# Block counts of the last layer: five cells per step beside each attention loop, in place of four and six

## What is computed

```python
x = _layernorm(x + L0(x, edge_index, edge_weight))       # weighted sum of neighbours
x = _layernorm(x + L1(x, edge_attr_32, edge_index, ...)) # attention, 4 heads, softmax over edges
x = _layernorm(x + L2(x, edge_index, ...))               # attention, 1 head, leaky relu
x = _layernorm(x + L3(x, edge_index, W1, b1, W2, b2))    # two graph convolutions:
# agg = segment_sum(x[col], row); agg/deg ; relu((agg/deg + x) @ W1 + b1), then again with W2
```

## Time and profile before

| what | us |
|---|---|
| median of 3 runs | 4830.54 (4828.19 to 4831.01) |
| the profiled execution | 4824.61, its span 4822.8 |
| first attention loop, from 1885 to 2980 | 1095 |
| second attention loop, from 3107 to 4440 | 1333 |
| everything else | 2394.8 |

### The profile page before, as it was taken

How to read it: one execution, slowest core, us unless ns; L and a number is a source line. 1 busy time by engine, 2 the same in 40 slices (tenths; PEclk the granted TensorE clock), 3 DMA queues, 4 the chain that set the end, 5 groups by cost and what they waited for, 6 DMA issues and landing times. The chain is left out here.

```text
span 4822.8 us, 75928 instructions
## 1 busy us (share of the span) xinstructions
PE 2356.4 (49%) x18851; PEld 1736.9 (36%) x18904; DVE 2781.6 (58%) x5419; ACT 647.4 (13%) x1473; POOL 2686.7 (56%) x2730
## 2 busy tenths in 40 slices
PE   0133333333306624666666665355555555555798
PEld 0023333333305513454544454233333333333232
DVE  8641111111118865777777777577877887877201
ACT  0001111111105410111111111011111111111000
POOL 0037777777745522777777774176666666663000
PEclk9955555555555555566666656555555555555899
DMA  0133334343315523555555552143333333332744
GB/s 21 38 123 124 125 122 130 126 129 123 114 36 109 107 47 85 140 144 148 143 147 147 143 146 78 42 102 94 94 95 91 91 97 92 94 95 60 275 170 168
DMA packets 533005, 537.07 MB, mean 111 GB/s; under 512 B 213790, under 2 KB 370324, under 8 KB 532618
## 3 DMA queue, kind: packets, MB, share of 16 engines
q1 hardware_dynamic: 243738, 289.79, 20.1%
q0 software_dynamic: 81072, 115.39, 10.7%
q10 hardware_dynamic: 208000, 130.01, 8.8%
HBM read 376.99 MB, written 159.58 MB: 111 GB/s over the span
## 5 line engine op out<-in xcount | busy, mean ns | idle before, releaser
L1381 POOL DMA_INDIRECT rows<-nodes_xl,id_slot x832 | 868.3, 1044 | 577.8 <-issue 240.9
L638 POOL DMA_INDIRECT msg_by_src<-message,place_slot x832 | 832.6, 1001 | 343.5 <-issue 252.8
L1381 POOL DMA_INDIRECT rows<-nodes_kv,id_slot x832 | 822.6, 989 | 339.8 <-issue 242.0
L1697 PE MATMUL counts_p<-hot_blocks 128*128 128x128 bf16 x2080 | 541.1, 413 | 362.3 <-DVE running_counts L1569 319.8
L599 PE MATMUL picked<-X,hotT 128*128 x1664 | 374.5, 423 | 674.2 <-issue 390.3
L599 PEld LDWEIGHTS picked<-X,hotT 128*128 128x128 f32 x1664 | 360.6, 331 | 688.0 <-issue 688.0
L560 DVE TENSOR_TENSOR message<-picked,w_dst 128x512 f32<-128x512 f32 x104 | 71.9, 691 | 845.7 <-ACT message L612 838.0
L1738 PE MATMUL sums<-parts,hot 128*128 128x68 bf16 (+1 forms) x4992 | 325.2, 251 | 374.9 <-DVE parts L1558 374.9
L1697 PEld LDWEIGHTS counts_p<-hot_blocks 128*128 128x128 bf16 x2080 | 277.5, 148 | 545.0 <-DVE running_counts L1569 339.1
L1738 PEld LDWEIGHTS sums<-parts,hot 128*128 128x128 bf16 x4992 | 311.8, 168 | 424.1 <-issue 424.1
L1569 DVE SCALAR_TENSOR_TENSOR running_counts<-running_counts,same_block,counts_p 128x128 f32<-128x128 f32 x1040 | 359.8, 346 | 171.0 <-DVE running_counts L1569 31.3
(11 more groups left out here) (343 smaller groups left out, 3606.2 us busy)
## 6 DMA issues: line engine op xcount, KB each, us to landing
adjacency<-running_counts ACTq DMA_DIRECT2D x1040, 64.0 KB
loc_all<-loc_by_cell SPq DMA_DIRECT2D x104, 512.0 KB
hotT<-hotT_by_step SPq DMA_DIRECT2D x208, 256.0 KB, 3.1
hot<-hot_by_step SPq DMA_DIRECT2D x208, 256.0 KB, 3.1
blocks<-adjacency SPq DMA_DIRECT2D x40, 1280.0 KB, 11.4
hot_by_step<-hot ACTq DMA_DIRECT2D x104, 256.0 KB, 2.0
hotT_by_step<-hotT ACTq DMA_DIRECT2D x104, 256.0 KB, 2.2
rows<-msg_by_src SPq DMA_DIRECT2D x312, 68.0 KB
```

The costliest lines, as they stand in the source:

```text
L638: pool.indirect_dma_start(out=msg_dram, out_offset=bass.IndirectOffsetOnAxis(ap=ids[:, s, t:t + 1], axis=0), in_=rows[:, s, t, :], in_offs ...
L1381: pool.indirect_dma_start(out=rows[:, j, t, :], out_offset=None, in_=table, in_offset=bass.IndirectOffsetOnAxis(ap=ids[:, j, t:t + 1], axis=0)
L1697: ins = nc.tensor.matmul(counts_p[:, q - HALVES[half][0], :], hot_b[:, r, 1, :, t], hot_b[:, r, 0, :, t], start=g == 0, stop=g == 1)
```

## The change

```diff
 BPER = -(-(GROUPS + NT * NT - 1) // STEPS)
-BFIRST, BSECOND = BPER * 2 // 5, BPER - BPER * 2 // 5
+BFIRST, BSECOND = BPER // 2, BPER - BPER // 2
 BCELLS = BPER * STEPS
```

## The result

The changed kernel takes 4863.14 us (median of 4 runs, 4860.63 to 4866.41) against 4830.07 before: a ratio of 1.0069, 95% interval 1.0052 to 1.0087. It is slower by 33 us, where 41 was forecast. The profiled execution has a span of 4859.8 us, 37.0 more than before.

What follows compares the result with a forecast made beforehand. VectorE and those it waits for were taken to bound the first loop, VectorE alone the second. First loop +89 us and second -48 gave +41, so 4871 us against the median 4830.5; range 4826 to 4892.

Steps and rivals of the forecast that it cites:

- first loop, H to T1: First loop, start of `held` (L1469) to end of the parts of s = 2 (L1558): +2.43 us per window.
- first loop, T1 to T0: First loop, end of the parts of s = 2 to end of those of s = 3: +1.25 us per window.
- first loop, T0 to H: First loop, end of the parts of s = 3 to the next `held`: mean 0.0 us per window.
- wait behind the scatters, first loop: First loop: chain's three of s = 2 wait for six counts queued behind 48 scatter matmuls, 1.67 us new.
- register load laid bare: First loop, before the rescale: its register load, now behind the chain, is no longer overlapped, +0.75 us per window.
- second loop, H to T1: Second loop, start of `held` to end of the parts of s = 2: -1.24 us per window.
- second loop, T1 to T0: Second loop, end of the parts of s = 2 to end of those of s = 3: -0.45 us per window.
- The two cases foretold there: First loop, before `held`: windows with 3.23 us of VectorE waiting change by -0.93 us, those with the branch stall +1.0.
- Slack that covers the cells: Rival, first loop: VectorE's 50.1 us of waits are slack that added cells may fill; 4804 us, chance 0.12.
- Work that just moves: Rival, first loop: six count matmuls are done when VectorE arrives, no new wait; about 4831 us, chance 0.15.
- A second piece that is dearer still at s = 0 and s = 1: Rival: added waits there, or a growing branch stall, cost another 0.3 to 1 us a window; 4878 to 4895, chance 0.10.
- The width: Rival, both loops: tables of 1280 elements run at one element per cycle, +330 us, 5160 us; chance 0.03.

Runs made afterwards that it cites:

- e6: Changed kernel, rescale ahead of the chain's second piece; at s = 2 chain's first piece ahead of splits, second piece's counts ahead of scatters: 4719.55 us, ratio 0.9770.
- e3b: Changed kernel with the rescale of s = 2 put ahead of the chain's second piece, a repeat run: ratio 1.0006 to the kernel before.
- e9: Changed kernel, at s = 2 chain's first piece between weighings and splits, second piece's counts ahead of scatters, last of four runs: ratio 0.9825 to the kernel before.
- The chain early: Changed kernel, at s = 2 chain's first piece ahead of splits, second piece's counts ahead of scatters; four runs: 0.9829, 0.9818, 0.9811, 0.9825 to the kernel before.

## Why the prediction was right, point by point

The steps, per window; before and after are means over the last 24 windows of each loop, worked out from the timeline. In the second loop H is the start of L1472, which writes `held` there:

| step | foretold | measured |
|---|---|---|
| first loop, H to T1 | +2.43 | +2.52 (22.44 to 24.95) |
| first loop, T1 to T0 | +1.25 | +1.25 (10.67 to 11.92) |
| first loop, T0 to H | 0.0 | -0.17 (8.57 to 8.40) |
| wait behind the scatters, first loop | 1.67 | 1.69 |
| the same wait, second loop | 1.2 to 1.6 | 1.69 |
| register load laid bare | 0.75 | 0.91 |
| second loop, H to T1 | -1.24 | -1.52 (27.91 to 26.39) |
| second loop, T1 to T0 | -0.45 | -0.40 (13.90 to 13.50) |
| second loop, T0 to H | -0.27 | -0.31 (9.56 to 9.25) |
| tables of 1280 elements | 822 ns | 822 ns |

*What bounds the loops.* That VectorE, not GpSimd, sets the first loop's pace was the choice on which the sign hung, and it held: the period rose by 3.55 us although a window of gathers takes 40.9.

*First loop.* The sum of 3.7 came to 3.6. Two small errors partly cancel: the load costs 1.09 us in every second window and 0.73 in the others (why it is dearer there is open), and T0 to H fell a little. The two cases foretold there are in the rows: in the windows with the branch stall VectorE comes last and there is hardly a wait left at L1469 (none at 2432.80), in the others most of the 12.8 us lie. The windows without the stall lost 0.95 us, as foretold (0.93); those with it gained 0.6, not 1.0, and that is why the mean is not 0.0.

*Second loop.* The mechanism was right and one term mis-sized, H to T1: 1.52 us saved, not 1.24. Where it went can be read in the rows. Before, the chain behind the maxima waited 0.74 us in every second window, where 0.36 is the rule; that is gone. A row of before, and one of after:

```profile
3618.57 0.35 DVE L1569 SCALAR_TENSOR_TENSOR running_counts<-running_counts,same_block,counts_p 128x128 f32<-128x128 f32 x1 [0.74 <-DVE top_m L1475]
```

```profile
3593.00 0.35 DVE L1569 SCALAR_TENSOR_TENSOR running_counts<-running_counts,same_block,counts_p 128x128 f32<-128x128 f32 x1 [0.38 <-DVE top_m L1475]
```

The waits named after `top_m` fall from 12.9 us in 23 windows to 8.5, 0.19 us a window. The second scan of the carries (L1485) waited 2.6 us in 11 of these windows and does not wait now, 0.11 us a window. The two together account for the 0.28 us that the forecast had too few. The wait behind the scatters grew to 1.69 us, a little beyond the 1.2 to 1.6 given for it, and T1 to T0 saved 0.40 in place of 0.45.

*The total.* 24 windows of 3.60 and -2.24 us give 86 - 54 = 32, near the 33 of the medians; the profiled execution grew by 37, since 6 came ahead of the first loop's first maximum and 3 between the loops, where the prediction had put nothing, and the first windows of the two loops gave 4 back. Against the forecast's 41, the second loop saved 6 us more and the first cost 3 less.

*The rivals.* Slack that covers the cells: out, the first loop's window grew by 3.55 us, more than the 2.86 of the cells' own work. Work that just moves: out, the wait is there with 1.69 us in every window, and e6 shows that it costs time. A second piece that is dearer still at s = 0 and s = 1: out, it waits 0.07 us there. The width: out, by 822 ns. The step between the columns that TensorE reads, which went from 8 to 10 elements in the first loop and from 12 to 10 in the second, cost nothing that can be seen: eight count matmuls took 2.04 us at a step of 8, six took 1.56 to 1.59 at 12 and take 1.58 to 1.60 at 10. The note on SBUF cachelines in the Trainium skill (SBUF - State Buffer) gives 8 bf16 elements as the distance that is free; no cost of going beyond it shows in these reads. How a read without a step would fare no run here shows.

## What to carry to other kernels

Equal work moved between two loops is not free: count what queue each moved piece joins and whether its size changes how the work is cut, since a cut makes a second place where two engines wait for each other, and where that falls behind a long queue on the other engine it costs more than the work. Before the split of work is tuned, look at where such a piece stands in the other engine's order: here two moves with no change of work were worth 146 us together, and with them the other split was the better one. A move that helps a loop in two pieces can hurt the one in a single piece, so it has to be checked in each loop by itself.

## What the runs showed of the hardware

In four of the six sets of runs of the experiments the kernel before took 6219 to 6239 us in place of 4830, 29% more. It is not the chip alone: chip number 10 stands in sets of both kinds. The engines' instructions are as long there as elsewhere (a count matmul has a mean of 414 ns in e3b as in the changed kernel at 4863 us, though the mean granted clock of the whole program is 0.564 and 0.59); what differs is the time between them. TensorE in e3b, in the picks of step s = 3 of the first loop:

```profile
2648.34 3.03 PE L1738 MATMUL sums<-parts,hot 128*128 128x68 bf16 x46 [4.22 <-DVE parts L1558]
...
2652.58 1.84 PE L1697 MATMUL counts_p<-hot_blocks 128*128 128x128 bf16 x6
...
2656.20 0.33 PE L1673 MATMUL picked<-q_parts,hotT 128*128 x3 [1.15 <-issue]
2657.62 0.32 PE L1673 MATMUL picked<-q_parts,hotT 128*128 x3 [1.10 <-issue]
2659.04 0.32 PE L1673 MATMUL picked<-q_parts,hotT 128*128 x3 [1.10 <-issue]
...
2666.84 0.21 PE L1673 MATMUL picked<-q_parts,hotT 128*128 x1 [0.50 <-issue]
```

The 24 picks, 1.5 us elsewhere, take 15 us, with gaps of 0.3 to 1.9 us that nothing in the profile explains. VectorE stands still at the same time (`remote`: the profile names no instruction as the releaser):

```profile
2669.18 1.31 DVE L1569 SCALAR_TENSOR_TENSOR running_counts<-running_counts,same_block,counts_p 128x128 f32<-128x128 f32 x3 [17.86 <-remote]
```

But its chain waits for the six counts and not for the picks, and by these rows the counts were done at 2652.58 + 1.84 = 2654.42. Elsewhere the chain starts 0.14 us behind them; here it starts 14.76 us behind them. The same stands where TensorE has no stalled work of its own. In e9 the scores are turned by 2604.72, and VectorE takes them up at 2619.03:

```profile
2604.32 0.40 PE L1707 MATMUL turn_p<-scaled_ident,scores 128*128 128x128 f32 x2
...
2619.03 0.41 DVE L1469 TENSOR_SCALAR held<-turn_p,be_col,lt_col 128x128 f32<-128x128 f32 x1 [12.60 <-remote]
```

So this is not simply VectorE waiting for a slow TensorE: both engines come late, VectorE in these rows 14 to 15 us after the work that it waits for is over in the record (in which PE's ends are modelled). The stall of the chain comes in nearly every window of both loops, behind the scatters. A slow supply of instructions or signals that arrive late would look so, but no run tested either. In such a set an edit of some tenths of a microsecond per window could not be timed at this place. The chain early showed 1.7 to 1.9% there; why it did is not shown.
